# Mixing layer of a two-layer kernel: normalising on ScalarE, biases written into the product banks, key products and outer products one step later

## The reference, cut to what matters

```
xn = layernorm(x)
x2 = x + (u @ w2.T + w2_b) + (fp6(xn) @ fp6(wf).T + ffn_bias)   # end of layer 1; u comes from the scan
xn = layernorm(x2)                                          # layer 2
k  = relu(xn @ Wk.T + bk)
kv = sum over the rows of k (x) v,  k_sum = sum of k      # v = xn @ Wv.T + bv
...                                                          # attention, feed-forward and output follow
```

## Time and profile before

| | us |
|---|---|
| median of 3 runs | 2377.07 (2376.37 to 2377.99) |
| the profiled execution | 2379.92 |
| its span, first to last instruction | 2378.3 |
| mean granted TensorE clock | 0.979 of full |
| mixing layer, first to last instruction (about) | 612 to 1548 |

### The profile page before, as it was taken

The page is one execution under the profiler, slowest core; times in us unless marked ns, Lnnn a source line. Parts: engine busy times, 40 slices in busy tenths (PEclk is TensorE's granted clock), DMA queues, the critical chain, the costliest instruction groups (busy, mean ns, idle before and its releaser), DMA issues. The chain is left out here.

```text
span 2378.3 us, 27697 instructions
## 1 busy us (share of the span) xinstructions
PE 2151.1 (90%) x9464; PEld 1663.1 (70%) x9464; DVE 1681.1 (71%) x3176; ACT 874.8 (37%) x1449; POOL 922.6 (39%) x966
## 2 busy tenths in 40 slices
PE   7999997799598888889988888769999999999997
PEld 6788886244377677667776776658877788777886
DVE  5575555677577777777777777457777677776775
ACT  3445555000123232323232333264445444454432
POOL 0030000444455555555455555204434344443443
PEclk9999999899799999999999999979999999999999
DMA  3244433788422222222232221041122211222110
GB/s 136 102 147 126 150 120 119 282 290 296 137 75 72 83 78 72 80 75 73 72 109 79 82 71 62 32 159 63 63 80 82 88 63 62 80 80 89 63 36 36
DMA packets 165461, 241.39 MB, mean 101 GB/s; under 512 B 19273, under 2 KB 93257, under 8 KB 164170
## 3 DMA queue, kind: packets, MB, share of 16 engines
q1 hardware_dynamic: 162760, 231.31, 29.0%
q10 hardware_dynamic: 2562, 8.32, 0.9%
HBM read 138.86 MB, written 100.73 MB: 101 GB/s over the span
## 5 line engine op out<-in xcount | busy, mean ns | idle before, releaser
L94 PE MATMUL bank<-e_ring,e_w_hi 128*128 128x512 f32 x512 | 207.3, 405 | 17.9 <-DVE e_ring L1402 16.6
L95 PE MATMUL bank<-e_ring,e_w_hi 128*128 128x512 f32 x512 | 205.7, 402 | 0.0
L1084 PE MATMUL bank<-d_kh,d_nat 128*128 128x512 f32 x768 | 195.7, 404 | 7.1 <-DVE d_kh L987 7.1
L1402 DVE TENSOR_TENSOR e_ring<-e_mixed,e_ring 128x512 fp32r<-128x512 f32 x128 | 95.9, 749 | 149.8 <-ACT e_ring L1300 149.8
L96 PE MATMUL bank<-e_ring,e_w_lo 128*128 128x512 f32 x512 | 201.0, 393 | 0.0
L827 POOL TENSOR_TENSOR d_xq<-d_xq,d_magic 128x512 f32<-128x512 f32 x64 | 93.4, 1460 | 211.7 <-DVE d_xq L983 211.7
L1283 POOL TENSOR_TENSOR e_x<-e_x,e_ff 128x512 f32<-128x512 f32 x64 | 82.5, 1288 | 236.5 <-DVE e_ff L1451 236.5
L1277 POOL TENSOR_TENSOR e_x<-e_x,e_beta 128x512 f32<-128x512 f32 x64 | 83.6, 1306 | 225.0 <-ACT e_y L1322 225.0
L1084 PEld LDWEIGHTS bank<-d_kh,d_nat 128*128 128x128 f32 x768 | 141.4, 191 | 36.3 <-issue 7.7
L878 POOL TENSOR_TENSOR d_kacc<-d_kacc,d_kr 128x512 f32<-128x512 f32 x64 | 82.6, 1291 | 166.1 <-ACT d_kr L925 166.1
L1331 ACT ACTIVATE e_kr<-bank 128x512 f32<-128x512 f32 x64 | 38.1, 595 | 291.6 <-PE bank L96 236.5
(11 more groups left out here) (209 smaller groups left out, 6491.3 us busy)
## 6 DMA issues: line engine op xcount, KB each, us to landing
b_xg<-in_L_attn_x SPq DMA_DIRECT2D x32, 512.0 KB, 4.7
scr_v<-b_vt SPq DMA_DIRECT2D x64, 256.0 KB, 2.7
scr_z<-b_zt SPq DMA_DIRECT2D x64, 256.0 KB, 2.1
c_z<-scr_z SPq DMA_DIRECT2D x64, 256.0 KB, 3.0
c_v<-scr_v SPq DMA_DIRECT2D x64, 256.0 KB, 3.4
scr_u<-c_v SPq DMA_DIRECT2D x64, 256.0 KB, 2.4
d_x<-in_L_attn_x SPq DMA_DIRECT2D x64, 256.0 KB, 2.7
d_ut_raw<-scr_u SPq DMA_DIRECT2D x32, 512.0 KB, 3.6
```

The costliest lines, as they stand in the source:

```text
L94: eng.matmul(out, lhs[hi], rhs[hi], start=first, stop=False)
L95: eng.matmul(out, lhs[hi], rhs[lo], start=False, stop=False)
L1084: mm = pe.matmul(BG[c][:, :], s[:, i, cols], r[:, j, :], start=M % NTB == 0 and i == j, stop=M % NTB == NTB - 1 and i == 1, skip_group_che ...
L1402: nc.vector.tensor_tensor(ring[slot][:, 1, kt, :], src, ring[slot][:, 0, kt, :].bitcast(F32), ALU.subtract).then_inc(lo_done, 1)
```

## The change

In phase_mix:
- ScalarE normalises: the input (normalise_input, in place of line 962) and the sums (normalise_sums, in place of line 1040), each as an activation Identity with a scale and a bias for each row; the bias is minus mean times rstd, computed once for the input (shift0, on VectorE) and for each tile on GpSimd (shift1, in place of the two copies).
- Biases: ScalarE writes the summed bias of layer 1 into bank BX (set_sums) and the key bias into bank BK (set_keys) before the products, which all run with start=False; two matmuls ahead of the loop open the banks. GpSimd's add_bias (840) and VectorE's addition of the key bias (1052) are gone; VectorE adds the loaded tile itself to the bank; ScalarE reads the keys with relu twice from the bank.
- Order: key products of tile N-2 (before: N-1) and outer products of tile N-3 (before: N-2) in step N; the loop is one step longer. VectorE's order is low_keys(N-3), prepare_tile(N+2), sum and statistics of N, low_n(N-1), low_q(N+1), rest of N. GpSimd's is add_keys(N-3), low_u, prepare_tile(N+2), rstd and shift of N. ScalarE's is keys(N-3), set_keys(N-2), high_u, take_turned(N-1), set_sums(N+1), normalise_sums(N), high_q(N+1), normalise_input(N+3).
- A third buffer xq; the load of x for slot N % 4 now waits for the sum of the tile that held it, and is issued behind the store of x2.

Outside of it: the project and scan phases raise a shared semaphore, VectorE issues one memset less in scan, and the second layer takes shift1 ready made.

```diff
-def split_products(eng, out, lhs, rhs, first, last):
+def split_products(eng, out, lhs, rhs, first, last, onto=False):
+
     hi, lo = 0, 1
-    eng.matmul(out, lhs[hi], rhs[hi], start=first, stop=False)
-    eng.matmul(out, lhs[hi], rhs[lo], start=False, stop=False)
-    return eng.matmul(out, lhs[lo], rhs[hi], start=False, stop=last)
+    eng.matmul(out, lhs[hi], rhs[hi], start=first, stop=False, skip_group_check=onto)
+    eng.matmul(out, lhs[hi], rhs[lo], start=False, stop=False, skip_group_check=onto)
+    return eng.matmul(out, lhs[lo], rhs[hi], start=False, stop=last, skip_group_check=onto)
...
-        def add_bias(N):
-            q = N % Q
-            pool.wait_ge(x_ld[q], N // Q * 16 + 16)
-            if N >= Q:
-                pool.wait_ge(x2_st[q], N // Q * 16)
-                pool.wait_ge(xn_done, N - Q + 1)
-            nc.gpsimd.tensor_tensor(x2[q][:, :], xs[q][:, :], res_bias[:, :], ALU.add).then_inc(xb_done, 1)
...
+        def add_keys(M):
+            b = M // NTB
+            pool.wait_ge(kr_done, M + 1)
+            if M:
+                pool.wait_ge(kacc_done, M)
+            nc.gpsimd.tensor_tensor(kacc[b][:, :], kacc[b][:, :], kr[M % 2][:, :], ALU.add).then_inc(kacc_done, 1)
...
+        for N in range(2):
+            prepare_tile(N)
+        for N in range(NT + 3):
+            if N >= 3:
+                add_keys(N - 3)
+            if N % 2 and N // 2 + 1 < NT // 2:
+                low_u(N // 2 + 1)
+            if N + 2 < NT:
+                prepare_tile(N + 2)
             if N < NT:
                 pool.wait_ge(stat, 3 * N + 3)
-                nc.gpsimd.tensor_tensor(rstd[p][:, :], var_eps[:, :], keep["neg_half"][:, 0:1], ALU.pow)\
+                nc.gpsimd.tensor_tensor(keep["rstd1"][:, N:N + 1], var_eps[:, :], keep["neg_half"][:, 0:1], ALU.pow)\
                   .then_inc(rstd_done, 1)
...
-            if N + 1 < NT:
-                add_bias(N + 1)
-            if N >= 1:
...
 
     def scalar(act):
         def high_u(pair):
             act.wait_ge(u_ld[pair % 2], pair // 2 * 16 + 16)
-            tile = ut[pair % 2]
-            nc.scalar.activation(tile[:, 0, :, :], u_raw[pair % 2][:, :, :], ACT.Copy).then_inc(u_hi, 1)
+            nc.scalar.activation(ut[pair % 2][:, 0, :, :], u_raw[pair % 2][:, :, :], ACT.Copy).then_inc(u_hi, 1)
 
         def high_q(N):
             act.wait_ge(q_full, N + 1)
             nc.scalar.activation(qt[N % 2][:, 0, :, :], BB[:, :].rearrange("p (k t) -> p k t", k=KT), ACT.Copy)\
               .then_inc(q_hi, 1)
 
+        def normalise_input(N):
+            act.wait_ge(x_ld[N % Q], N // Q * 16 + 16)
+            if N >= 3:
+                act.wait_ge(q_full, N - 2)
+            nc.scalar.activation(xq[N % 3][:, :], xs[N % Q][:, :], ACT.Identity, scale=keep["rstd0"][:, N:N + 1],
+                                 bias=shift0[:, N:N + 1]).then_inc(xq_done, 1)
+
+        def set_sums(N):
+
+            if N:
+                act.wait_ge(x2_done, N)
+            nc.scalar.activation(BX[:, :], res_bias[:, :], ACT.Copy).then_inc(x2_set, 1)
+
+        def set_keys(M):
+
+            if M:
+                act.wait_ge(k_hi, M)
+            nc.scalar.activation(BK[:, :], bk[:, :], ACT.Copy).then_inc(k_set, 1)
+
+        def keys(M):
+            act.wait_ge(k_full, M + 1)
+            if M >= 2:
+                act.wait_ge(kacc_done, M - 1)
+                act.wait_ge(k_lo, M - 1)
+            nc.scalar.activation(kr[M % 2][:, :], BK[:, :], ACT.Relu).then_inc(kr_done, 1)
+            if M >= 2:
+                act.wait_ge(outer_done, M - 1)
+            nc.scalar.activation(kh[M % 2][:, 0, :], BK[:, :], ACT.Relu).then_inc(k_hi, 1)
+
+        def take_turned(M):
+            act.wait_ge(n_full, M + 1)
+            if M >= 4:
+                act.wait_ge(n_lo, M - 3)
+                act.wait_ge(xt_st[M // 2 % 2], M // 4 * 16)
+            nc.scalar.activation(turned(M), BA[:, :].rearrange("p (k t) -> p k t", k=KT), ACT.Copy).then_inc(n_copy, 1)
+            act.wait_ge(n_copy, M + 1)
+            if M >= 2:
+                act.wait_ge(k_full, M - 1)
+            nc.scalar.activation(nt[M % 2][:, 0, :, :], turned(M), ACT.Copy).then_inc(n_hi, 1)
+
+        def normalise_sums(N):
+            act.wait_ge(norm_done, N + 1)
+            act.wait_ge(x2_done, N + 1)
+            if N >= 2:
+                act.wait_ge(n_full, N - 1)
+                act.wait_ge(nat_lo, N - 1)
+            nc.scalar.activation(xn[N % 2][:, :], x2[N % Q][:, :], ACT.Identity, scale=keep["rstd1"][:, N:N + 1],
+                                 bias=keep["shift1"][:, N:N + 1]).then_inc(xn_done, 1)
+            act.wait_ge(xn_done, N + 1)
...
+        for N in range(NT + 3):
+            if N >= 3:
+                keys(N - 3)
+                if N - 2 < NT:
+                    set_keys(N - 2)
+            if N % 2 == 0 and N // 2 + 1 < NT // 2:
+                high_u(N // 2 + 1)
+            if 1 <= N <= NT:
+                take_turned(N - 1)
+            if N + 1 < NT:
+                set_sums(N + 1)
+            if N < NT:
+                normalise_sums(N)
             if N + 1 < NT:
                 high_q(N + 1)
-            if N < NT:
-                act.wait_ge(xn_done, N + 1)
-                if N >= Q:
...
+        def prepare_tile(N):
+            tile, p = xq[N % 3], N % 2
+            blocks = tile[:, :].rearrange("p (b e) -> p b e", e=QBLOCK)
             at = PREP * N
-            dve.wait_ge(x_ld[q], N // Q * 16 + 16)
+            dve.wait_ge(xq_done, N + 1)
+            nc.vector.tensor_reduce(q_max[:, :], blocks, AX.X, ALU.max, apply_absolute_value=True).then_inc(prep, 1)
+            dve.wait_ge(prep, at + 1)
             if N >= 2:
-                dve.wait_ge(q_full, N - 1)
-            nc.vector.tensor_scalar(xq[p][:, :], xs[q][:, :], keep["mean0"][:, N:N + 1], keep["rstd0"][:, N:N + 1],
-                                    ALU.subtract, ALU.mult).then_inc(prep, 1)
-            dve.wait_ge(prep, at + 1)
-            nc.vector.tensor_reduce(q_max[:, :], blocks, AX.X, ALU.max, apply_absolute_value=True).then_inc(prep, 1)
-            if between is not None:
-                between()
-            dve.wait_ge(prep, at + 2)
+                dve.wait_ge(q_done, N - 1)
             nc.vector.tensor_scalar(q_scale[:, p, :], q_max[:, :], 1.0 / FP6_MAX, SCALE_EPS, ALU.mult, ALU.max)\
               .then_inc(prep, 1)
+            dve.wait_ge(prep, at + 2)
+            nc.vector.reciprocal(q_inv[:, :], q_scale[:, p, :]).then_inc(prep, 1)
             dve.wait_ge(prep, at + 3)
-            nc.vector.reciprocal(q_inv[:, :], q_scale[:, p, :]).then_inc(prep, 1)
-            dve.wait_ge(prep, at + 4)
...
+
+        def sums(N):
+            p, q = N % 2, N % Q
+            dve.wait_ge(x2_full, N + 1)
+            if N >= Q:
+                dve.wait_ge(x2_st[q], N // Q * 16)
+                dve.wait_ge(xn_done, N - Q + 1)
+            nc.vector.tensor_tensor(x2[q][:, :], BX[:, :], xs[q][:, :], ALU.add).then_inc(x2_done, 1)
+            dve.wait_ge(x2_done, N + 1)
+            nc.vector.bn_stats(stats[:, :], x2[q][:, :]).then_inc(stat, 1)
+            dve.wait_ge(stat, 3 * N + 1)
+            nc.vector.memset(keep["beat"][:, :], 0.0)
+            if N >= 2:
+                dve.wait_ge(norm_done, N - 1)
+            nc.vector.bn_aggr(moments[p][:, :], stats[:, :]).then_inc(stat, 1)
+            dve.wait_ge(stat, 3 * N + 2)
+            if N:
+                dve.wait_ge(rstd_done, N)
+            nc.vector.tensor_scalar(var_eps[:, :], moments[p][:, 1:2], LN_EPS, None, ALU.add).then_inc(stat, 1)
+
+        def low_nat(N):
+            q = N % Q
+            dve.wait_ge(nat_hi, N + 1)
+            nc.vector.tensor_tensor(nat[q][:, 1, :], xn[N % 2][:, :], nat[q][:, 0, :].bitcast(F32),
+                                    ALU.subtract).then_inc(nat_lo, 1)
 
         def sums_row(b):
...
+            if N + 2 < NT:
+                prepare_tile(N + 2)
             if N < NT:
-                dve.wait_ge(x2_full, N + 1)
-                dve.wait_ge(xb_done, N + 1)
-                nc.vector.tensor_tensor(x2[q][:, :], BX[:, :], x2[q][:, :], ALU.add).then_inc(x2_done, 1)
-                dve.wait_ge(x2_done, N + 1)
-                nc.vector.bn_stats(stats[:, :], x2[q][:, :]).then_inc(stat, 1)
-                dve.wait_ge(stat, 3 * N + 1)
-                nc.vector.memset(keep["beat"][:, :], 0.0)
-                nc.vector.bn_aggr(moments[p][:, :], stats[:, :]).then_inc(stat, 1)
-                dve.wait_ge(stat, 3 * N + 2)
-                nc.vector.tensor_scalar(var_eps[:, :], moments[p][:, 1:2], LN_EPS, None, ALU.add).then_inc(stat, 1)
+                sums(N)
+            if 1 <= N <= NT:
+                low_n(N - 1)
             if N + 1 < NT:
                 low_q(N + 1)
             if N < NT:
-                dve.wait_ge(rstd_done, N + 1)
-                if N >= 2:
-                    dve.wait_ge(n_full, N - 1)
```

(90 more changed lines are left out.)

134 lines of the change are left out of this document (43 added, 91 removed).

## The result

| | before | changed |
|---|---|---|
| median, us | 2377.15 | 2333.37 (2330.72 to 2335.48) |
| ratio to before, 95% interval | | 0.9818 (0.9806 to 0.9829) |
| profiled execution, us | 2379.92 | 2332.52 |
| its span, us | 2378.3 | 2330.9 |

The account below looks back on a forecast made before the run. The prediction took a loop through every engine, for which TensorE waits, as the bound. 31 pairs at 1.38 us take 42.8 from the profiled 2379.92; less 2.85 to the median gives 2334, range 2290 to 2356 (the forecast's own 2315 to 2352).

Parts of the forecast that it names:

- The old loop is cut: Mixing layer: prepare_tile(N+2) ahead of the sum on VectorE ends TensorE's wait for GpSimd's tile, 53.0 us in 47 steps.
- The loop that takes its place: Mixing layer: a loop without TensorE, through ScalarE, VectorE and GpSimd, sets the step, 12.38 us from kr without low_u.
- q_scale behind low_u, 1.54 us: Steps with low_u: VectorE's q_scale is held until GpSimd's low_u ends at 4.86, adding 1.54 us to the loop.
- rstd beside low_n, 0.99: GpSimd's rstd, 0.55 us alone, takes 0.99 because VectorE's low_n with two SBUF inputs runs beside it.
- Bank writes at nothing: ScalarE's set_keys and set_sums fall into waiting time and are not on the loop.
- Products one step later change nothing: Key and outer products one step later on TensorE change no rate.
- The sum: A pair of steps takes 26.30 us against 27.68, 1.38 less; over 31 pairs 42.8 us.
- the ends: Fill, end of the first batch and the extra last round: 0, with 5 us on either side.
- take the place of waits: After the last sum, one more round of keys and outer products replaces waits already there, taken as 0.
- The slower rival: VectorE's q_scale or scaling is caught by GpSimd's key sum every step, 0.60 us a step over before: 2414; chance 0.08.
- TensorE's floor: TensorE's own products and transposes in the mixing layer take 12.08 us a step.
- rival 2: q_scale escapes low_u too, so TensorE becomes the bound: 109 us less, 2268; chance 0.08.

Follow-up runs that it names:

- e10: Kernel before with only VectorE's order changed: prepare_tile(N+2) ahead of the sum of tile N, low_n behind it, low_keys at the end; 2386.4 us, ratio 1.0040.
- e11: Changed kernel with prepare_tile back at the end of VectorE's step; on GpSimd behind shift and low_u (even steps), key sum last; 2282.8 us, ratio 0.9604.
- e1: Changed kernel with GpSimd's low_u moved to the end of the even step, behind the shift; 2291.6 us, ratio 0.9643.
- e2: Changed kernel with VectorE's low_n waiting until GpSimd has made rstd and shift of the step; 2308.2 us, ratio 0.9712.
- e6: Changed kernel with xn made on VectorE again, the input still normalised on ScalarE; 2296.7 us, ratio 0.9668.
- e7: Changed kernel with each of ScalarE's two bank writes made twice; 2331.7 us, ratio 0.9817.
- e8: Changed kernel without the bank write into BX; GpSimd adds the bias of the sums behind the shift; 2334.9 us, ratio 0.9829.
- e5: Changed kernel with the later products undone: key products of N-1, outer products of N-2, loop one step shorter; 2332.9 us, ratio 0.9823.
- e9: Changed kernel with GpSimd's key sum waiting for low_keys; 2338.9 us, ratio 0.9846.
- e4: Changed kernel with low_n waiting for rstd and shift, and GpSimd's key sum, then low_u (even steps), behind the shift; 2271.0 us, ratio 0.9557.

## Why the prediction was right

- **The old loop is cut.** Right: TensorE's wait for line 829 is gone from the waits, and pairs fell from 27.68 to 26.29. The prediction credits this to the order. The order alone does cut it (e10), but the kernel isn't faster by that, and with the other edits and GpSimd's new order the old loop doesn't bind even with prepare_tile at the end (e11).
- **The loop that takes its place.** Right, term by term. From kr, predicted and measured in the step without low_u: end of low_keys 2.56 and 2.50; q_scale 3.20 and 3.14; end of prepare_tile 6.02 and 5.98; GpSimd done 8.49 and 8.47; rstd done 9.48 and 9.43; xn 9.79 and 9.83 (the shift takes 0.27 rather than 0.18); next kr 12.38 and 12.40. That this is the loop and not a list of idle coincidences is shown by e1, e2 and e6: each takes a known length out of it, and 42, 25 and 37 us come off.
- **q_scale behind low_u, 1.54 us.** Measured 1.66 against 0.18, and the two steps differ by 1.48. e1 takes it away. The prediction let low_u start when low_keys lets go, at 2.48, and run 2.38. Its row starts at 1.92, right behind the key sum, and is 2.85 long; it ends at 4.77 where the sum has 4.86, so the term is right.
- **rstd beside low_n, 0.99.** Measured 1.00; with low_n out of the way it is 0.55 (e2). The Trainium skill's rule (SBUF — State Buffer, "Who interferes with whom") that the blocked side waits for the whole of the other would have put up to 0.69 there. In this trace low_n itself waits first (from 918.25, with its 0.69 of work only after line 826's reads are over), and starts before 826's row has ended, so 0.45 remains. The rows decide; the kind of collision is as the rule says.
- **Bank writes at nothing.** Right (e7, e8), at 0.60 us each.
- **Products one step later change nothing.** Right in the steps and in the whole (e5); fill, batch end and the end of the layer each change, see below.
- **The sum.** 31 pairs at 1.38 gave 42.8 of span; it fell by 47.4. Not all of this is the loop. Between the first and the last sum of the layer the time fell from 875.2 to 822.2 us, 53.0, of which 63 steps at 0.695 are 43.8 and the other 9 lie in the first three steps (3), at the end of the first batch (2) and in the last two steps (4), which take 9.78 and 12.04. The first sum comes 4.4 earlier (633.46 against 637.83). But from the last sum to the second layer's first instruction it is 44.7 us instead of 35.5. (The 0.8 left is in the other phases.) The prediction set the ends to 0 with 5 on either side: all up to the last sum was 13.6 better than the steps alone, and the tail 9 worse, and the two nearly cancel. The one more round of outer and key products behind the last sum does not "take the place of waits"; it brings waits of its own. TensorE waits for low_keys three times there, 2.24, 2.67 and 2.67 us; e5, with one round fewer, has two such waits and a tail of 35.0. That part of the agreement is luck. So is the rest of it: the profiled execution of before lies 2.8 us above its median and that of the changed kernel 0.9 below, so the span fell by 47.4 where the medians fell by 43.8.
- **The slower rival** was priced wrongly. It added the whole of the key sum's 1.29 us to the loop, where q_scale is held for 0.65 (0.83 for 0.18), and didn't take off the 0.71 that the same key sum no longer costs low_keys (0.69 for 1.40); e9 has 5.5 us over the change in place of 80.
- **TensorE's floor.** Read as 12.08, it is 12.045 in e4, and 2271 is the time there; 2268 was named as rival 2.
